# First quarter of a block's expert products ahead of the last tile's back product, in two halves, the second quarter in another bank, and transposes between later quarters

## What is computed

```python
x = x + gnn(layernorm(x), edge_attr, edges)            # gather, segment sum, two dense layers with batch norm, silu
x = x + mixture(layernorm(x))

# mixture: groups of t = 16 rows; 16 experts e, 4 sets s, inner width f = 32, d = 512
grouped = x.reshape(B, S // 16, 16, D)
logits = einsum('bgtd,des->bgtes', grouped, controller) + tie
perm = (logits == max(logits, axis=-3, keepdims=True))   # one row of each group for each (e, s)
intermediate = einsum('bgtd,desf->bgtesf', grouped, f1)
inner = relu(einsum('bgtesf,bgtes->bgesf', intermediate, perm))
inter2 = einsum('bgesf,esfd->bgesd', inner, f2)
result = einsum('bgesd,bgtes->bgtd', inter2, perm)
```

## Time and profile before

| | |
|---|---|
| median of 3 runs | 2023.17 us (2020.66 to 2024.76) |
| the profiled execution | 2016.82 us |
| its span | 2015.1 us |
| PE busy | 1842.8 us, 91% |
| DVE, ACT, POOL busy | 59%, 49%, 18% |
| last 17 of 40 slices, PE | nine tenths or more in all |

### The profile page before, as it was taken

One profiled execution on the slowest core, in us unless ns is written; L12 is line 12 of the kernel. 1 busy time (PEld: TensorE's weight loads), 2 busy tenths in 40 slices (PEclk: granted clock), 3 DMA queues, 4 the chain that ended last, 5 costly groups with the idle time before them and its releaser, 6 DMA issues. The chain is left out here.

```text
span 2015.1 us, 41123 instructions
## 1 busy us (share of the span) xinstructions
PE 1842.8 (91%) x15824; PEld 1350.1 (67%) x15824; DVE 1187.9 (59%) x2345; ACT 988.8 (49%) x1715; POOL 362.8 (18%) x428
## 2 busy tenths in 40 slices
PE   5486599999999979999999968999999999999999
PEld 3354478888888858888888865656666566666554
DVE  6486466666666443333333265766767767667665
ACT  2355123333333265565565344656656657556553
POOL 4486220000000000000000042222222222222210
PEclk9678799999999989999999999999999999999999
DMA  9987755566666353343343174534444435344322
GB/s 367 293 146 102 173 163 163 163 184 183 182 176 170 112 193 123 129 170 128 122 169 136 56 270 152 153 117 127 142 127 133 142 112 157 116 128 137 106 76 69
DMA packets 162346, 305.66 MB, mean 152 GB/s; under 512 B 15418, under 2 KB 87098, under 8 KB 159003
## 3 DMA queue, kind: packets, MB, share of 16 engines
q1 hardware_dynamic: 153240, 282.66, 44.5%
q0 software_dynamic: 8960, 20.98, 5.5%
HBM read 168.72 MB, written 134.87 MB: 151 GB/s over the span
## 5 line engine op out<-in xcount | busy, mean ns | idle before, releaser
L1434 PE MATMUL bank<-f2s,inner_bd 128*32 128x512 f32 x2528 | 297.2, 597 | 4.6 <-issue 3.7
L1318 ACT ACTIVATE inter_hi<-bank 128x512 fp32r<-128x512 f32 x316 | 189.1, 598 | 194.8 <-PE bank L1434 192.4
L571 ACT ACTIVATE h1o<-bank,b_by_channel 128x500 f32<-128x500 f32 x160 | 108.7, 679 | 327.1 <-PE bank L386 327.1
L384 PE MATMUL bank<-ahi,w_hi 128*128 128x500 f32 x640 | 250.8, 392 | 14.4 <-DVE alo L725 14.4
L1240 DVE TENSOR_TENSOR inter_lo<-bank,inter_hi 128x512 fp32r<-128x512 f32 x316 | 216.3, 690 | 78.7 <-ACT inter_hi L1318 77.7
L384 PE MATMUL bank<-hhi,w_hi 128*128 128x500 f32 x640 | 251.5, 393 | 2.7 <-DVE hlo L532 2.7
L386 PE MATMUL bank<-hhi,w_lo 128*128 128x500 f32 x640 | 249.9, 390 | 0.0
L385 PE MATMUL bank<-hlo,w_hi 128*128 128x500 f32 x640 | 249.5, 390 | 0.0
L385 PE MATMUL bank<-alo,w_hi 128*128 128x500 f32 x640 | 249.2, 389 | 0.0
L386 PE MATMUL bank<-ahi,w_lo 128*128 128x500 f32 x640 | 248.9, 389 | 0.0
L538 DVE BATCH_NORM_STATS2 stats<-h1o 128x500 f32 (+1 forms) x160 | 103.6, 676 | 162.9 <-ACT h1o L571 162.9
(11 more groups left out here) (133 smaller groups left out, 3188.6 us busy)
## 6 DMA issues: line engine op xcount, KB each, us to landing
h1T<-h1o SPq DMA_DIRECT2D x19, 2000.0 KB, 8.1
h1in<-h1T SPq DMA_DIRECT2D x19, 2000.0 KB, 9.6
aggregate<-zeros SPq DMA_DIRECT2D x20, 1024.0 KB, 9.1
x<-in_x SPq DMA_DIRECT2D x79, 256.0 KB, 2.6
x<-x SPq DMA_DIRECT2D x79, 256.0 KB, 3.4
x_back<-x SPq DMA_DIRECT2D x79, 256.0 KB, 2.9
out<-x_back SPq DMA_DIRECT2D x79, 256.0 KB, 2.1
h2in<-h2T SPq DMA_DIRECT2D x39, 512.0 KB, 4.2
```

The lines of the kernel that those rows point to most:

```text
L384: nc.tensor.matmul(out, w_hi[:, k, cols], a_hi[:, k, :], start=(k == 0), stop=False)
L571: nc.scalar.activation(h1o[b][:, m, :], mb[m % 4][:, 0:CW], ACT.Identity, bias=b1c[:, m:m + 1]).then_inc(evr, 1)
L1318: nc.scalar.activation(ihi[n % QB][:, :], bI[n % QB][:, :], ACT.Copy).then_inc(ihr, 1)
L1434: last = nc.tensor.matmul(bI[b][32 * i:32 * i + 32, :], ibd[:, e, j, :, :].rearrange("p s g -> p (s g)"), f2s[:, e, :], start=True, stop=True)
```

## The change

- `inner` 0 moves in `schedule` from the end of the body to its last tile, ahead of `final` and `result`. In the first body, which has no back half, its place stays the same.
- Every quarter now runs its contraction in two halves of two chunks. For quarter 0 the first half waits for two yT evictions fewer than the second. The start and stop flags are adapted; the number of matmuls stays.
- Quarter q goes to `bQ[q]`: bank 2, bI[2], bank 2, bank 3. The waits follow: quarter 1 no longer waits for the last tile's result (`otr`), quarter 3 does; quarter 2 waits for the relu of quarter 0 as before, quarter 3 no longer for that of quarter 1.
- At tile 0 of a body with a back half, `norm` 2 moves ahead of unit 0 (it was behind its low part), and `turn_x` 2 moves from behind the sums of tile 0 to between unit 1 and quarter 3.

```diff
+        bQ = [bD[0], bI[2], bD[0], bD[1]]
@@ schedule, tile 0 with a back half
                 if behind and m == 0:
                     yield "inner", 1
+                    if next_:
+                        yield "norm", m + 2
                     yield "unit", u
                     yield "low", u
-                    if next_:
-                        yield "norm", m + 2
                     if new:
                         yield "turn_g", m + 3
                     yield "inner", 2
...
                     yield "low", u + 1
                     if new:
                         yield "stats", m + 3
+                    if next_:
+                        yield "turn_x", m + 2
                     yield "inner", 3
...
                     if ahead:
                         yield "sums", m
-                    if next_:
-                        yield "turn_x", m + 2
@@ schedule, end of a tile
+                last = m == max(tiles(front), tiles(back)) - 1
+                if last and front is not None:
+                    yield "inner", 0
                 if behind:
                     yield "final", m
                     yield "result", m
-            if front is not None:
-                yield "inner", 0
@@ relu
-                      bD[q % 2][32 * s:32 * s + 32, ...
+                      bQ[q][32 * s:32 * s + 32, ...
@@ inner
-                    if q == 0:
-                        if static(k, 1):
-                            pe.wait_ge(wf1, 16 * KH)
-                        pe.wait_ge(yr, (k * TB + tiles(k)) * KH)
-                    else:
-                        if q == 1 and not static(k, 1):
-                            pe.wait_ge(otr, k * TB)
-                        if q >= 2:
-                            pe.wait_ge(inv, (k * QB + q - 1) * 2)
-                            pe.wait_ge(ina, (k * QB + q - 1) * 2)
-                    for e in range(QE * q, QE * q + QE):
-                        for c in range(KH):
-                            for s in range(NS):
+                    if q == 0 and static(k, 1):
+                        pe.wait_ge(wf1, 16 * KH)
+                    if q == 1 and not static(k, 1):
+                        pe.wait_ge(ilr, unit_of(k, 0))
+                    if q == 2:
+                        pe.wait_ge(inv, (k * QB + 1) * 2)
+                        pe.wait_ge(ina, (k * QB + 1) * 2)
+                    if q == 3 and not static(k, 1):
+                        pe.wait_ge(otr, k * TB)
+                    for half in range(2):
+                        if q == 0:
+                            done = (k * TB + tiles(k)) * KH
+                            pe.wait_ge(yr, done if half or static(k, 1) else done - KH // 2)
+                        for e in range(QE * q, QE * q + QE):
+                            for c in (2 * half, 2 * half + 1):
+                                for s in range(NS):
...
+                                        start=(c == 0 and e % QE == 0), stop=(c == KH - 1 and e % QE == QE - 1))
```

More of the change, by code:

```diff
@@ L1009, in schedule @@
                     yield "result", m
-            if front is not None:
-                yield "inner", 0
         def relu(op, q, s, *more):
             return op(ibd[32 * s:32 * s + 32, QE * q:QE * q + QE, :, s, :],
-                      bD[q % 2][32 * s:32 * s + 32, 0:QE * TB * GB].rearrange("p (e j g) -> p e j g", e=QE, g=GB), *more)
+                      bQ[q][32 * s:32 * s + 32, 0:QE * TB * GB].rearrange("p (e j g) -> p e j g", e=QE, g=GB), *more)
         def unit_of(kb, u):
@@ L1450, in inner @@
                 def inner(k, q):
-                    if q == 0:
-                        if static(k, 1):
-                            pe.wait_ge(wf1, 16 * KH)
-                        pe.wait_ge(yr, (k * TB + tiles(k)) * KH)
-                    else:
-                        if q == 1 and not static(k, 1):
-                            pe.wait_ge(otr, k * TB)
-                        if q >= 2:
-                            pe.wait_ge(inv, (k * QB + q - 1) * 2)
-                            pe.wait_ge(ina, (k * QB + q - 1) * 2)
-                    for e in range(QE * q, QE * q + QE):
-                        for c in range(KH):
-                            for s in range(NS):
[L1465 to L1469, removed]
+                    if q == 0 and static(k, 1):
[14 more added lines that the diff above has]
+                                for s in range(NS):
+                                    es = e * NS + s
+                                    last = nc.tensor.matmul(
+                                        bQ[q][32 * s:32 * s + 32, (e % QE) * 64:(e % QE) * 64 + 64],
+                                        f1s[:, c, es * FF:(es + 1) * FF], yT[:, c, es, :],
+                                        start=(c == 0 and e % QE == 0), stop=(c == KH - 1 and e % QE == QE - 1))
                     last.then_inc(inp, 1)
```

## The result

The changed kernel takes 2015.38 us (median of 7 runs, 2012.59 to 2016.96) against 2021.36 (7 runs, 2018.88 to 2024.76): a ratio of 0.9968 (95% interval 0.9957 to 0.9979), 6.5 us faster. On another chip it gave 0.9972 (0.9961 to 0.9982). The forecast was 8.5 us. The profiled execution took 2014.11 us with a span of 2012.3.

What follows compares the result with a forecast made beforehand. The prediction took PE to bound the mixture, stalled at block ends by instruction fetch. Its terms, 7.97 + 1.8 - 1.3 = 8.5 us, off the median 2023.17 gave 2014.7 us, range 2009.5 to 2021.5.

Steps and rivals of the forecast that it cites:

- The stalls are instruction fetch: At a block's end PE stops within quarters because the next piece of 256 instructions has not landed; no size of its own.
- Stall 1: PE's stop within quarter 1: gone from blocks 1 to 9, as the next piece is requested earlier; 7.97 us gained.
- The later stalls: Stops after quarter 1's: they stay, but the sequencer meets the second crossing ahead of PE; 1.8 us gained (0 to 5).
- Stalls 2 and 3: PE's stops in quarters 2 and 3: arrivals and landings both move earlier, so they stay and the gain is kept.
- the first rival: Store and residual load, some 2 us later, delay the second crossing's packets; gain only 0 to 2, say 2022 us; chance 0.12.
- The transposes: Moved ahead of quarter 3: covered in either place, but eight instructions push the later crossing by four records; 1.3 us lost.
- In block 0 nothing moves: Block 0 has no `final` there, so it was to gain nothing.
- about 11: Sign of being right: PE's idle "issue" time ahead of the expert products falls from 22.8 to about 11 us.

Runs made afterwards that it cites:

- the shift of 16 records for 32 instructions: The kernel before with 64 long-met waits of PE put once at the mixture's start: 2023.27 us in one run.
- the store held too: The changed kernel, and one with only quarter 0 moved, SP holding tile 0's loads and the last result's store until quarter 3: 0.9868 and 0.9866.
- Holding the loads alone: The changed kernel, but SP holds the load of x tile 4 and all behind it until quarter 3: 2003.34 us, ratio 0.9895.
- the kernel with `norm` back: The changed kernel with `norm` 2 put back behind the low part of unit 0: 2014.89 us, ratio 0.9954.
- run 128: Not a label of a run: the words say that PE can execute 128 matmul records, with 128 weight loads, in 1.99 us.

## Why the prediction was right, and where it was not

- **The stalls are instruction fetch**: right, by the shift of 16 records for 32 instructions, and by the packet that ends 1.2 to 1.6 us ahead of each restart. The Trainium skill's "mostly hidden" ("Runtime: NRT & Kernel Launch", "Instruction fetch mechanics") doesn't hold in this kernel: its blocks of 256 instructions are there, but the crossings cost PE over 20 us.
- **Stall 1, 7.97 us**: right, and for the reason given: the packet starts 1.6 us earlier in block 6 (1.86 worked out). The gap is gone from all nine blocks; quarter 1's gaps sum to 0 in every kernel with quarter 0 ahead, and to 5.8, 6.9 and 7.9 us in those without.
- **The later stalls, +1.8 us for the sequencer's lead**: the term that failed, in sign too. In the change quarter 2's gaps grew by 1.5 us over seven blocks (2.3 in the second profile). A lead seems to exist: by an estimate (counted back 127 records from the gap in quarter 2) the second packet starts 0.7 and 0.5 us after PE enters the piece in blocks 6 and 7, where after a stop it is 1.1. What it is worth isn't shown. With the store held too, quarter 2's gaps are 1.3 and 0.8 us against 2.4 before, but no run holds the store with quarter 0 in its old place.
- **"Stalls 2 and 3 stay and the gain isn't given back"**: the failed step behind most of the difference. I had treated a fetch period as a property of PE's side. It also depends on what is queued on the DMA engines when the request comes. I had noted that SP's x load would come about 1 us sooner and priced it at nothing; the first rival had the mechanism, but named only the store and the second packet. The loads and the third packet cost more: quarter 3's gaps grew by 3.3 us where the transposes should have shortened them by 7 x 0.5. Holding the loads alone took 8.8 us off them.
- **The transposes, -1.3 us**: that they gain nothing, since the yT wait grows, was right to a tenth of a microsecond (4.3 to 9.1 us). Their price couldn't be told apart from zero (0.9868 against 0.9866; `norm` differs in its place between these two as well).
- **"In block 0 nothing moves"**: wrong. The stretch of block 0 is 2.9 us shorter in the profile, 2.1 of it in quarter 3, where the earlier `norm` has the loads out of the way of the packet sooner. It is the mechanism that cost time in the other blocks.
- **The sum**: of 8.5 forecast, 6.0 to 6.5 were measured. In the profiles the 7.97 came as worked out, and in blocks 1 to 7 quarters 2 and 3 gave back 4.8 where 3.9 less (seven transposes) and 1.4 less (the lead) was forecast, so that blocks 1 to 8 gained only 0.6 us over all. What is left comes from block 9 (2.2) and block 0 (2.9). That the total came near the forecast is thus in part luck, and so is the nearness of the times, 2015.38 to the forecast's 2014.7: before's median fell by 1.8 us with more runs. The prediction's sign "about 11" for the idle time ahead of the products doesn't follow from its own terms either, 22.8 - 6.3 - 4.5 = 12.0.
- The kernel with quarter 0 alone (0.9957, 8.7 us by its ratio) has the forecast's size, and `norm` and `turn_x` alone cost 6.7 us by theirs; together they give 6.5, so the parts don't add up. With quarter 0 ahead the earlier loads do less harm; why is not shown.
- Not settled: whether the changed kernel is slower than quarter 0 alone. 0.9968 and 0.9972 against 0.9957 and 0.9954, with intervals that overlap. The second timing of the change came out at the 0.997 that was expected if the others are really faster, but a difference of 0.0015 is within what each of their ratios is uncertain by. What the kernel with `norm` back saves in quarter 3 it loses in two long waits.

## What to carry to other kernels

An idle engine with no releaser, inside a run of short instructions with no wait in the code, is worth counting: if the gaps recur every 256 instructions and each ends behind an instruction packet, the engine is being fed its program too slowly, and what helped here is to lay slow instructions between fast ones and to keep bulk transfers off the DMA engines at that time. When a reordering makes one engine's step earlier, list the transfers which that step releases and what else is asking for the DMA engines then. A stall filled with work is only a gain if the place from which the work was taken doesn't turn into a wait.

## What the runs showed of the hardware

- PE can run 128 matmul records and 128 weight loads in 1.99 us, but a piece of 256 instructions takes 3.82 us from one stall's end to the next with the loads held (block 4), and 5.45 us behind data that keep the 16 DMA engines 97% busy.
- After a stop the packet starts some 1.1 us later when nothing is ahead of it. It carries 16 KB, and PE goes on 1.2 to 1.6 us after it has ended (48 of 49 stops in the profiles of before and of the change).
- Two plain waits in a row were packed into one instruction (64 waits made 32 instructions).
